# Kernel study: a layer norm's reciprocal root from ScalarE and one Newton step in place of an integer guess and three

## The reference

```python
def _layernorm(x, axis=-1, eps=1e-5):
    m = jnp.mean(x, axis=axis, keepdims=True)
    v = jnp.var(x, axis=axis, keepdims=True)
    return (x - m) / jnp.sqrt(v + eps)
...
    # layer 0: mean of the neighbours, two dense maps, relu
    h = jnp.maximum(_layernorm(x, axis=-1), 0.0)
    x = x + _L0_gnn_ref(h, adj, L0_gnn_W_self, L0_gnn_b_self, L0_gnn_W_nb, L0_gnn_b_nb, L0_gnn_W_comb, L0_gnn_b_comb)
    # layer 1: attention over the neighbours, 8 heads
    h = jnp.maximum(_layernorm(x, axis=-1), 0.0)
    x = x + _L1_gnn_ref(h, adj, L1_gnn_W, L1_gnn_a)
    # layer 2: attention, 4 heads, quaternion weights, elu
    h = jnp.maximum(_layernorm(x, axis=-1), 0.0)
    x = x + _L2_gnn_ref(h, adj, L2_gnn_W, L2_gnn_a)
    # layer 3: attention, 1 head
    h = jnp.maximum(_layernorm(x, axis=-1), 0.0)
    x = x + _L3_gnn_ref(h, adj, L3_gnn_W, L3_gnn_a1, L3_gnn_a2)
    return x
```

## Time and profile before

| | |
|---|---|
| runs | 1273.11, 1275.97, 1277.37 us; median 1275.97 |
| profiled execution | 1273.54 us; span from first to last instruction 1270.0 us |
| busy: PE, DVE, POOL, ACT | 926.5, 862.3, 684.2, 394.6 us |
| scan and preparation | 0 to 324 us |
| layers 0, 1, 2, 3 | from 324, 550, 810 and 1047 us |
| mean granted TensorE clock | 0.874 of full |

### The profile page before, as it was taken

The page is one execution under the profiler, slowest core; times in us unless marked ns, Lnnn a source line. Parts: engine busy times, 40 slices in busy tenths (PEclk is TensorE's granted clock), DMA queues, the critical chain, the costliest instruction groups (busy, mean ns, idle before and its releaser), DMA issues.

```text
span 1270.0 us, 12232 instructions
## 1 busy us (share of the span) xinstructions
PE 926.5 (73%) x2854; PEld 500.0 (39%) x2854; DVE 862.3 (68%) x2786; ACT 394.6 (31%) x1200; POOL 684.2 (54%) x648
## 2 busy tenths in 40 slices
PE   3985979999076477639999998478878853747774
PEld 1332433444055355514555556234344431313332
DVE  3867699920386898718787875188889963747563
ACT  3552656632032143312323223133344440101110
POOL 4043413373677777347777500477775007777773
PEclk9987989999588699979999999787788965868888
DMA  9999967622776788546577501365775015656662
GB/s 360 374 350 357 329 254 294 222 72 73 231 240 192 231 282 251 173 142 187 164 201 209 160 33 42 100 188 163 208 212 166 34 51 152 177 142 180 183 183 85
DMA packets 81446, 242.73 MB, mean 191 GB/s; under 512 B 16931, under 2 KB 19395, under 8 KB 77275
## 3 DMA queue, kind: packets, MB, share of 16 engines
q0 software_dynamic: 47488, 144.09, 40.0%
q1 hardware_dynamic: 33882, 97.82, 21.0%
HBM read 203.00 MB, written 53.64 MB: 202 GB/s over the span
## 4 chain that ended last, share of the span: by engine, by line
PE 30%; DVE 25%; POOL 14%; DMA 12%; issue 12%; ACT 5%; POOLq 1%; SPq 0%; ACTq 0%
POOL arena L1067 10%; PE psum L666 9%; PE psum L689 8%; PE psum L625 6%; DVE arena L1358 4%; DVE arena L1299 4%; PE psum L735 3%; DMA arena<-T,arena 3%; DMA arena<-XV,arena 2%; ACT arena L781 2%; DVE arena L1178 2%; DMA arena<-in_L_gnn_a 2%; DMA arena<-in_adj 2%; DVE arena L1116 2%; PE psum L603 2%
## 5 line engine op out<-in xcount | busy, mean ns | idle before, releaser
L1067 POOL DMA_INDIRECT arena<-T,arena x476 | 514.2, 1080 | 365.4 <-issue 179.1
L689 PE MATMUL psum<-arena,misc 128*128 128x512 f32 x476 | 255.8, 663 | 65.4 <-DVE arena L1358 65.4
L666 PE MATMUL psum<-arena 128*128 128x264 f32 (+1 forms) x832 | 223.2, 414 | 46.9 <-ACT arena L781 46.9
L625 PE MATMUL psum<-arena 128*128 128x512 f32 (+1 forms) x416 | 198.3, 619 | 30.4 <-ACT arena L794 17.3
L666 PEld LDWEIGHTS psum<-arena 128*128 128x128 f32 (+1 forms) x832 | 164.2, 202 | 124.8 <-ACT arena L781 72.5
L603 PE MATMUL psum<-misc,arena 128*128 128x128 f32 (+1 forms) x520 | 88.0, 295 | 142.5 <-ACT arena L765 80.4
L1358 DVE TENSOR_TENSOR arena<-arena 128x512 f32<-128x512 f32 x238 | 161.2, 685 | 1.8
L765 ACT ACTIVATE arena<-arena 128x512 f32<-128x512 f32 x104 | 84.7, 815 | 245.9 <-DVE arena L1275 229.2
L689 PEld LDWEIGHTS psum<-arena,misc 128*128 128x128 f32 x476 | 95.4, 212 | 155.8 <-issue 122.3
L603 PEld LDWEIGHTS psum<-misc,arena 128*128 128x128 f32 (+1 forms) x520 | 65.5, 151 | 194.1 <-ACT arena L765 91.7
L735 PE MATMUL psum<-arena 128*128 128x512 f32 (+1 forms) x208 | 117.3, 716 | 17.8 <-ACT arena L778 17.8
(11 more groups left out here) (137 smaller groups left out, 990.0 us busy)
## 6 DMA issues: line engine op xcount, KB each, us to landing
arena<-in_adj SPq DMA_DIRECT2D x25, 1663.5 KB, 8.5
T<-arena SPq DMA_DIRECT2D x75, 260.0 KB, 3.5
arena<-T,arena POOLq DMA_INDIRECT x476, 3.8
T<-arena SPq DMA_DIRECT2D x25, 256.0 KB, 2.7
XV<-arena SPq DMA_DIRECT2D x25, 256.0 KB, 2.3
PW<-arena POOLq DMA_DIRECT2D x5, 1024.0 KB, 8.5
arena<-in_x SPq DMA_DIRECT2D x1, 3072.0 KB, 17.4
XV<-arena SPq DMA_DIRECT2D x1, 3072.0 KB, 21.4
```

The source lines that it names most:

```text
L625: last = e.matmul(p_own[which][0:n, :], HT[t % 2][:, k, 0:n], W0[which][:, k, :], start=k == 0, stop=k == 3 and which == 0)
L666: last = e.matmul(p_wh[0:n, a, :], ht[:, k, 0:n], WL[l][:, k, a, :], start=k == 0, stop=k == 3)
L689: e.matmul(p_num[s % 3].rearrange("p (a o) -> p a o", a=2), ident, halves(GB[:, BASE[l, s] + k, :])[:, :, 0:HALF], start=k == 0, stop=k == ...
L1067: e.indirect_dma_start(GB[:, BASE[l, s] + k, 0:ROW], None, dr["T"][l], bass.IndirectOffsetOnAxis(ap=(IDP if l else IDX)[:, t, k:k + 1], ax ...
```

## The change

The norm of layers 0 to 2's output (`norm`) gets its guess from ScalarE: Ln of -2hv and Exp of minus half of it, both on a [128, 1] column, in a new step `guess` in ScalarE's list. In layer 0's loop it stands just ahead of `new_h`, behind HT of the tile before. In the loop of layers 1 and 2 it stands behind the exponential (and the ELU passes) and ahead of the copy of products or scores, of HT and of `new_h`. VectorE waits for it and does one Newton step in two instructions. The function table is loaded explicitly ahead of the scan. `first_norm` keeps its guess and three steps.

```diff
+        e.preload_act_table_set("natural_log_exp_and_others")
         mark(0)
...
+        def guess(l, s):
+
+            m = (l + 1) * NT + s
+            st = small[m % 2]
+            e.wait_ge(S["var"], l * NT + s + 1)
+            e.activation(st[:, 16:17], st[:, 13:14], ACT.Ln, scale=-2.0).then_inc(S["logs"], 1)
+            e.wait_ge(S["logs"], l * NT + s + 1)
+            e.activation(st[:, 15:16], st[:, 16:17], ACT.Exp, scale=-0.5).then_inc(S["guess"], 1)
+
...
             if r - 1 < NT:
+                guess(0, r - 1)
                 new_h(0, r - 1)
...
+                if 0 <= r - 3 < NT:
+                    guess(l, r - 3)
                 if 0 <= r - 5 < NT:
...
-        def rsqrt(chain, y, var, hv, t, free=None):
-
-            chain.wait()
-            chain(e.tensor_scalar(hv, var, 1e-5, -0.5, ALU.add, ALU.mult))
-            yield
-            chain.wait()
-            if free:
-                e.wait_ge(S["h"], free)
-            chain(e.tensor_scalar(y.bitcast(I32), hv.bitcast(I32), -0.5, GUESS, ALU.mult, ALU.add))
-            yield
-            for _ in range(3):
-                chain.wait()
-                chain(e.tensor_scalar(t, hv, y, y, ALU.mult, ALU.mult))
-                yield
-                chain.wait()
-                chain(e.tensor_scalar(y, t, 1.5, y, ALU.add, ALU.mult))
-                yield
...
-            yield from rsqrt(ln, st[:, 8:9], st[:, 7:8], st[:, 13:14], st[:, 14:15], m - 1)
+            y, hv, guess, u = (st[:, c:c + 1] for c in (8, 13, 15, 14))
+            ln.wait()
+            e.tensor_scalar(hv, st[:, 7:8], 1e-5, -0.5, ALU.add, ALU.mult).then_inc(S["var"], 1)
+            yield
+            e.wait_ge(S["guess"], l * NT + s + 1)
+            ln(e.tensor_scalar(u, hv, guess, guess, ALU.mult, ALU.mult))
+            yield
+            ln.wait()
+            e.wait_ge(S["h"], m - 1)
+            ln(e.tensor_scalar(y, u, 1.5, guess, ALU.add, ALU.mult))
+            yield
```

## The result

| | before | after |
|---|---|---|
| median of 20 runs, us | 1275.79 (1268.39 to 1281.38) | 1285.47 (1276.78 to 1289.86) |
| ratio of the runs | | 1.0074, 95% interval 1.0057 to 1.0092 |
| profiled execution, us (its span) | 1273.54 (1270.0) | 1289.22 (1285.7) |
| issues of indirect DMAs in layer 0, busy us | 153.15 | 164.64 |

The changed kernel is slower by 9.7 us in the medians.

The account below looks back on a forecast made before the run. Bound by GpSimd in layer 0, TensorE in layer 1, a serial path in layer 2's pairs and VectorE in its last six; 0.8 + 0.6 - 2.8 + 4.8 - 0.4 = 3.0 us gained, 1273.0 us, range 1265.5 to 1279.5.

Parts of the forecast that it names:

- Covered.: Layer 0: GpSimd sets the pace with a lead of up to 32 slots, so the moved guess costs nothing.
- Rival C: Layer 0: VectorE counts there too; 0.5 us a norm over twelve norms gives 6 us, total 1267; chance 9%.
- Layer 0's end: End of layer 0: H ready near 526 us, TensorE free at 528.1; gain of 0.8 us.
- Layer 1's start: Start of layer 1: four half steps less between gathering and H; gain of 0.6 us.
- Layer 2, pairs: Layer 2 until about 979 us: ScalarE's two passes add 0.35 us to each of eight pairs; loss of 2.8 us.
- Last six: Layer 2's last six full iterations, bound by VectorE: 39.6 us in place of 45.2, less 0.8; gain of 4.8 us.
- the ring: Layer 2's last six: weights, variance, guess, score copy, store, H, exponential, back to the weights; 6.5 us an iteration.
- The end: Layer 2's end, three norms without multiplications: guess, copy, store and H take back the gain; loss of 0.4 us.
- Scan: Scan: table loaded at once, first mark maybe 1.3 us sooner, second waits for a DMA; 0, at most 1.3 us.
- A: Layer 2's pairs fall into another phase, TensorE at full clock in a third; 6 us more gained, 1267; chance 20%.
- B: Layer 2's last six: a store of 3.7 us makes iterations 8.1 us, 3.4 lost; total 1282, slower; chance 12%.
- D: ScalarE's function table is swapped, two loads in each of 78 norms, 200 us; total 1450; chance 1%.

Follow-up runs that it names:

- two0: Kernel before, with layer 0 putting two of the norm's small operations behind each add in place of three, against the kernel before: ratio 1.0066, issues 159.9 us.
- one0: Kernel before, with one Newton step of three in layer 0's norm (less exact), against the kernel before: ratio 0.9997, issues 157.4 us.
- apart0: Changed kernel, with an add between variance and the operation waiting for the guess in layer 0; ratio to the kernel before 1.0042, issues 161.4 us.
- psum_after: Changed kernel, with the running sum of layer 0's adds in PSUM in place of SBUF; ratio to the kernel before 0.9907, issues 148.2 us.

## Why the prediction was wrong, point by point

**The step that failed is layer 0: "Covered."** I weighed whether VectorE or ScalarE would be late for GpSimd there, and they are not: GpSimd waits for neither by more than 3 us in all, before or after. What I took as given was its own turn, "one each 1.37 us". That number held a loss of 0.06 us an issue to VectorE's adds, which it escaped for the rest by walking in step with them. The change broke the step: fewer small pieces behind an add (two0 and one0 show that alone, +6.8 and +4.3 us of issues) and an add started whenever the guess arrives (without that wait, in apart0, the issues take 3.2 us less than in the changed kernel). Together they make +11.5 us, in the one stage where GpSimd sets the pace; how these divide between the two is not shown. Rival C looked at the same stage and the wrong side: it let VectorE give time back. No rival had GpSimd slowed.

**Layer 0's end, a gain of 0.8:** not seen. From the last issue to the last H it took 15.6 us and takes 17.5; over all kernels of the normal chips it is 13.4 to 17.1 without the change in this layer and 14.2 to 17.5 with it.

**Layer 1's start, a gain of 0.6:** the first H comes 3.0 us sooner after the last of layer 0, but the third only 0.56 (60.87 us, now 60.31): the size is right in this trace, but the third H lies anywhere from 59.6 to 62.7 us in the others. **Layer 1's steady part, 0:** right. The usual two iterations take 17.1 us before and after; the 2.4 us by which layer 1 is longer from first to last H are the early first H, most of which is lost again by the third.

**Layer 2, pairs, a loss of 2.8:** right in this trace. From the weights of tile 0 to those of tile 19 it took 165.0 us and takes 168.2; the passes are 0.2 us each, as taken. By H, the first 18 iterations took 154.7 to 156.1 us in the six normal traces with the old norm and 154.2 to 158.8 in the six with the early place.

**Last six, a gain of 4.8:** 45.18 us before, 39.98 now, a gain of 5.2. The size was right, and that is in part luck: I had H released by the store, and it waits for the shift (line 1280) in five of the six and for the store once (1.76 us). The store was as fast as taken, median 2.0 us; an iteration took 6.7 us, where I had 6.5 to 6.8 by the ring and 6.2 to 6.8 by VectorE's own path. **The end, a loss of 0.4:** from the end of that stretch to the last H it took 12.3 us and takes 13.8: a loss of 1.5.

**Scan, 0 to 1.3 gained:** its end is 2.8 us later. On chips of the usual speed it ends at 321.6 to 325.7 us (mean 323.7) in five traces without the early table load and at 323.3 to 329.5 (mean 325.9) in ten with it. That may be a cost of 2 us, or scatter; no run takes the load alone, so it stays open.

**VectorE's busy time:** 801.4 us where I said 775. Of 390 operations 60.9 us went, 0.156 each. The busy time counts overlapping work once, so it shows the 0.15 us that one was worth on a full path and not its 0.27 or 0.21. The section of "VectorE: DVE Perf Modes" in the Trainium skill that the prediction quotes says in the same paragraph that an operation which is not held starts earlier; the prediction left that out, so the nine multiplications in 5.50 us do not speak against the page. **ScalarE:** +29.7, said 31.

**A, B, D:** none happened. Layer 2's granted clock is 0.79 where it was 0.80, the last six's store stayed at 2.0 us, one table load.

So five terms (both of layer 1, all three of layer 2) came out within 1.1 us in this one pair of traces, and the median still missed by 12.5, of which the issues of layer 0 are 11.5 in the trace. The range took its width from waits and never asked whether an engine that waits for nobody can itself be slowed.

And in layer 2 I priced the wait I saw (the variance, then the guess, then the score copy) but took the change's order as given. My ring came to 6.5 us because of that order; with the passes late the last six take 35.3 us by H, not 39.1.

## What to carry to other kernels

Where one engine issues without a gap and sets a stage's pace, ask what lengthens its single instruction, not only what it waits for: compare its shortest with its mean duration, and see which other engine is busy in the long ones. Small operations between wide ones can be what keeps two engines out of each other's way; a sum kept in PSUM took the conflict away (0.75 us an add in place of 0.74), while fewer or more small pieces only moved it. When a pass that needs another engine's result enters an in-order list, put it behind everything that is already ready, even where that makes its own reader wait.

## What the runs showed of the hardware

- An indirect DMA's issue on GpSimd takes 1.00 us, and up to 1.54 when a 512-wide VectorE instruction with two SBUF inputs that began before it is still running 0.12 us after its start: it then ends 0.88 us behind the add. What counts is that moment, not the overlap: an add that begins with the issue and runs beside it for 0.7 us costs nothing. The Trainium skill, "SBUF — State Buffer", section on the two separate sides, says that whoever starts first keeps the shared ports for its whole instruction. For the add that agrees; for the issue it does not: an add that begins within an issue takes its usual 0.74 us.
- An add that begins 0.03 to 0.1 us before an issue either holds it or is itself lengthened, to 0.81 us at most in the kernels before and after and to 0.80 in one0.
- An add whose running sum is in PSUM takes 0.75 us, as against 0.74 with SBUF, and costs the issue nothing: 57 issues that fell on one in psum_after took 1.005 us on average.
- A pair of engines with turns of 1.31 and 1.34 us stayed in step by itself (the kernel before, 8.1 us lost in 145 issues); with turns of 1.31 and 1.10 behind most adds (two0) they lost 14.9.
- Two chips took 1428 and 1450 us for a kernel that takes 1276 on the others, with pauses of 9 to 16 us on several engines. What causes them was not looked into.
